# A template's bands loaded as 16-bit halves in six transfers, a first pass ahead of the loop, and a triangular mask by selection

## The reference, cut to what matters

```python
# 1. tokens: normalized template matching, one map per image
norm_t = ((flat - mu) / (sd + EPS)).reshape(C, th, tw) / patch_elements   # 31x31 template per channel
result = _dw_conv2d(image, norm_t[:, None], 1, pad)                       # correlation
m1, m2 = _dw_conv2d(image, mean_kern), _dw_conv2d(image * image, mean_kern)
result = (result / (sqrt(m2 - m1 * m1) + EPS)).mean(axis=1)
result = jnp.where(jnp.isnan(result), 0, result)                          # [16, 256, 256]
# 2. h = layernorm(h + attention(h)): 256 tokens of width 256 an image, 16 query and 8 key heads of 64
sim = tanh(q @ k.T / 50) * 50 / 8;  sim = where(causal, -max, sim);  out = softmax(sim) @ v
# 3. h = layernorm(h + ffn(h)): silu(x w1) * (x w2), two gelu layers of 1024, and back to 256
```

## Time and profile before

| | us |
|---|---|
| median of three runs | 2039.68 |
| profiled execution, its own time | 2037.89 |
| its span in the profile | 2036.2 |
| PE busy | 1841.0 (90%) |
| DVE busy | 1184.6 (58%) |
| ACT busy | 876.8 (43%) |
| POOL busy | 473.1 (23%) |
| PE in the first 80 us, by stretches of ten | 0, 3.0, 2.3, 10.0, 0.9, 1.9, 10.0, 1.9 |

### The profile page before, as it was taken

How to read it: one execution, slowest core, us unless ns; L and a number is a source line. 1 busy time by engine, 2 the same in 40 slices (tenths; PEclk the granted TensorE clock), 3 DMA queues, 4 the chain that set the end, 5 groups by cost and what they waited for, 6 DMA issues and landing times. The chain is left out here.

```text
span 2036.2 us, 31526 instructions
## 1 busy us (share of the span) xinstructions
PE 1841.0 (90%) x11768; PEld 1585.8 (78%) x11768; DVE 1184.6 (58%) x2083; ACT 876.8 (43%) x1076; POOL 473.1 (23%) x376
## 2 busy tenths in 40 slices
PE   3699999999969989998998999699999999999997
PEld 2698988988957877777787778578778787777876
DVE  6788788888865786776678676323241423414141
ACT  3655654545525764664576466122221222222221
POOL 2100000000022231221232123133433324333342
PEclk8799999999998999998999999799999999999999
DMA  8131222224001002000200100150000000000000
GB/s 168 49 128 49 96 78 90 76 99 143 22 32 63 23 15 77 24 15 9 85 23 15 56 22 22 49 223 14 8 21 0 21 0 21 21 0 21 0 11 12
DMA packets 17240, 96.81 MB, mean 48 GB/s; under 512 B 3270, under 2 KB 3398, under 8 KB 11209
## 3 DMA queue, kind: packets, MB, share of 16 engines
q1 hardware_dynamic: 17100, 94.90, 13.9%
HBM read 82.27 MB, written 24.15 MB: 52 GB/s over the span
## 5 line engine op out<-in xcount | busy, mean ns | idle before, releaser
L556 PE MATMUL conv<-w_hi,x_hi 128*128 128x368 f16 (+5 forms) x1320 | 355.8, 279 | 4.2 <-DVE planes L452 4.2
L556 PE MATMUL conv<-w_lo,x_hi 128*128 128x368 f16 (+5 forms) x1320 | 356.2, 279 | 0.0
L556 PE MATMUL conv<-w_hi,x_lo 128*128 128x368 f16 (+5 forms) x1320 | 355.0, 279 | 0.0
L818 POOL TENSOR_TENSOR probs<-probs,mask 128x512 f32<-128x512 f32 x128 | 166.8, 1303 | 444.1 <-ACT probs L892 444.1
L1310 ACT ACTIVATE raw_c<-ring,sh 128x512 f32<-128x512 f32 x128 | 88.2, 689 | 370.3 <-PE ring L1407 370.3
L1098 PE MATMUL mixed<-v,probs 128*128 128x65 f32 x1536 | 202.9, 283 | 41.5 <-DVE parts L978 41.5
L1098 PEld LDWEIGHTS mixed<-v,probs 128*128 128x128 f32 x1536 | 187.2, 197 | 56.8 <-issue 40.0
L1407 PE MATMUL ring<-ha_hi,wh 128*128 128x512 f32 x512 | 208.2, 407 | 16.9 <-POOL ha_lo L1272 16.9
L1272 POOL TENSOR_TENSOR ha_lo<-raw_c,ha_hi 128x512 fp32r<-128x512 f32 x128 | 165.0, 1289 | 210.1 <-DVE ha_hi L1322 210.1
L1407 PE MATMUL ring<-ha_lo,wh 128*128 128x512 f32 x512 | 205.4, 401 | 0.0
L1322 DVE CAST ha_hi<-raw_c 128x512 fp32r<-128x512 f32 x128 | 80.7, 631 | 212.9 <-ACT raw_c L1310 210.7
(11 more groups left out here) (148 smaller groups left out, 3563.7 us busy)
## 6 DMA issues: line engine op xcount, KB each, us to landing
xt<-x_columns_in SPq DMA_DIRECT2D x12, 1163.0 KB, 5.3
xp<-x_patches_in SPq DMA_DIRECT2D x12, 1152.0 KB, 5.2
hidden_words<-hidden_weights_in SPq DMA_DIRECT2D x8, 1408.0 KB, 8.2
words<-hidden_words SPq DMA_DIRECT2D x32, 352.0 KB, 3.1
wh<-hidden_words SPq DMA_DIRECT2D x2, 4096.0 KB, 21.1
tokens<-planes SPq DMA_DIRECT2D x4, 1024.0 KB, 3.9
lines<-tokens SPq DMA_DIRECT2D x4, 1024.0 KB, 5.4
h<-tokens SPq DMA_DIRECT2D x4, 1024.0 KB, 7.4
```

The lines of the kernel that those rows point to most:

```text
L556: ins = pe.matmul(out, xs[:, c, RI - 1 - i:RI - 1 - i + NR, :, x].rearrange("p r g -> p (r g)"), w, start=(t == 0), stop=(t == len(terms) ...
L818: pool.tensor_tensor(diag, diag, both, ALU.mult).then_inc(s_mask, 1)
```

## The change

It does four things.

1. The padded template is made as two 16-bit arrays of 47 rows of 64 (hi, and lo by a second DVE instruction), placed in the first 3 partitions of x_hi and x_lo, stored in two DMAs, and spread by six loads (one for each channel and half) over 128 partitions by 5,088 bytes. The casts on ACT and the subtractions on POOL go. Channel 0's two loads come before the loads of plane 1's image, channels 1 and 2 after them. The rows of a band in SBUF are 64 elements apart, not 48.
2. PE's `first()` runs the whole first group: in plane 0 correlate(0,0,0) comes after half of the turns, and the turns of plane 1 are moved back behind quarters 2 and 3; the loop begins at group 1. The order of the first pass on DVE and ACT changes with it, and POOL clears `lines` only after the template is normalized.
3. The mask is two selections of 256 columns (affine_select) in place of one product of 512.
4. `valid` is 16-bit.

```diff
-TROWS, TCOLS = TH + 16, TH + 32
+TROWS, TCOLS = TH + 16, TH + 33
+BAND = RI * PR * TCOLS
...
-            sp.wait_ge(s_tdve, 6)
-            sp.dma_start(TPAD, tpad).then_inc(s_tpad, 16)
-            sp.wait_ge(s_tpad, 16)
-            for c in range(CHANNELS):
-                for a in range(PR):
-                    size = (RI * PR - 1) * TCOLS + CJ * PC
-                    src = bass.AP(tensor=TPAD.tensor, offset=c * TROWS * TCOLS + a * TCOLS, ap=[[1, PC], [1, size]])
-                    sp.dma_start(spread[a * PC:(a + 1) * PC, c, 0:size], src).then_inc(s_wraw[c], 16)
+            for k in range(2):
+                sp.wait_ge(s_tdve, 6 + k)
+                sp.dma_start(TPAD[k], tpad[k]).then_inc(s_tpad, 16)
+            sp.wait_ge(s_tpad, 32)
+
+            def load_bands(c):
+                size = (RI * PR - 1) * TCOLS + CJ * PC
+                for k, w in enumerate((w_hi, w_lo)):
+                    src = bass.AP(tensor=TPAD.tensor, offset=(k * CHANNELS + c) * TROWS * TCOLS,
+                                  ap=[[TCOLS, PR], [1, PC], [1, size]])
+                    sp.dma_start(w[:, c, 0:size], src).then_inc(s_band[c], 16)
...
             def first():
+                load_bands(0)
                 load_xt(0, 1, 1)
                 load_x(0, 1, 1)
+                load_bands(1)
+                load_bands(2)
                 load_xt(0, 2, 2)
...
             def first():                      # ACT
                 square(0)
-                regroup(0)
                 split_hi(0, 0)
-                bands(0)
-                act.wait_ge(s_const, 5)
+                regroup(0, 0)
+                act.wait_ge(s_const, 7)
                 turned(0, 0)
-                turned(0, 1)
+                regroup(0, 1)
                 square(1)
                 mean_square(0)
-                bands(1)
-                regroup(1)
-                bands(2)
+                turned(0, 1)
+                regroup(1, 0)
+                act.wait_ge(s_tpad, 32)
                 deviation(0)
+                regroup(1, 1)
...
             def first():                      # DVE
                 sum_down(0, 0)
+                split_lo(0, 0)
                 sum_down(0, 1)
-                split_lo(0, 0)
-                dve.wait_ge(s_tpad, 16)
                 sum_across(0, 0)
+                sum_down(1, 0)
                 sum_across(0, 1)
-                sum_down(1, 0)
                 variance(0)
                 sum_down(1, 1)
-                dve.wait_ge(s_wlo, CHANNELS)
+                dve.wait_ge(s_tpad, 32)
...
             def first():                      # PE
-                turn_sums(0, range(8))
+                turn_sums(0, range(4))
+                correlate(0, 0, 0)
+                turn_sums(0, range(4, 8))
+                correlate(0, 0, 1)
+                correlate(0, 0, 2)
+                turn_sums(1, range(4))
+                correlate(0, 0, 3)
+                turn_sums(1, range(4, 8))
+                for c in range(1, CHANNELS):
+                    body(0, c, c, False)
...
-                        diag = probs[:, n % 4].rearrange("p m (b i) -> p m b i", b=3)[:, :, 0:3:2]
-                        both = mask[:].rearrange("p (m b i) -> p m b i", m=1, b=1).to_broadcast([P, 2, 2, P])
-                        pool.tensor_tensor(diag, diag, both, ALU.mult).then_inc(s_mask, 1)
+                        settle(pool, s_settle)
+                        for jb in range(2):
+                            diag = probs[:, n % 4, :, 2 * jb * P:(2 * jb + 1) * P]
+                            ins = pool.affine_select(out=diag, in_=diag, compare_op=ALU.is_ge, fill=0.0, base=0,
+                                                     pattern=[[0, 2], [1, P]], channel_multiplier=-1)
+                        ins.then_inc(s_mask, 1)
```

More of the change, by code:

```diff
@@ L106, in token_stage @@
         eps_t = sb("eps_t", [P, 1])
[L107 to L108 removed]
+        w_hi = sb("w_hi", [P, CHANNELS, BAND], F16)
+        w_lo = sb("w_lo", [P, CHANNELS, BAND], F16)
+        bands = lambda w: w[:].rearrange("p k (i a w) -> p k i a w", i=RI, a=PR)
         xp = sb("xp", [P, XW])
@@ L119, in token_stage @@
         guess = sb("guess", [P, PR, SIDE])
-        planes_4 = sb("planes_4", [P, 4, PR, SIDE])
-        valid, part, rinv, total = (planes_4[:, k] for k in range(4))
+        valid = sb("valid", [P, PR, SIDE], F16)[:]
+        planes_3 = sb("planes_3", [P, 3, PR, SIDE])
+        part, rinv, total = (planes_3[:, k] for k in range(3))
         tmpl = part[0:CHANNELS].rearrange("p a c -> p (a c)")[:, 0:TAPS]
         tsq = part[0:CHANNELS].rearrange("p a c -> p (a c)")[:, TAPS:2 * TAPS]
[L125 to L128, removed]
+        tpad = [x[0:CHANNELS, 1:].rearrange("p k r g c -> p (k r g c)")[:, 0:TROWS * TCOLS] for x in (x_hi, x_lo)]
         conv = psum("conv", [P, 4, 512])
@@ L138, in token_stage @@
         s_tpad = sem("s_tpad")
-        s_wraw = [sem("s_wraw%d" % c) for c in range(CHANNELS)]
-        s_whi = sem("s_whi")
-        s_wlo = sem("s_wlo")
+        s_band = [sem("s_band%d" % c) for c in range(CHANNELS)]
         s_xp = sem("s_xp")
@@ L165, in token_stage, with planes @@
         LAST = GROUPS * CHANNELS - 1
-        def planes(eng, body, first):
+        def planes(eng, body, first, start=0):
             first()
-            with eng.Fori(0, GROUPS - 1) as g:
+            with eng.Fori(start, GROUPS - 1) as g:
                 for c in range(CHANNELS):
@@ L235, in _ @@
         def _(pool):
+            for k in range(2):
+                pool.memset(tpad[k], 0.0).then_inc(s_const, 1)
+            pool.memset(eps_t[:], EPS_T).then_inc(s_const, 1)
             pool.memset(ident[:], 0.0).then_inc(s_const, 1)
-            pool.memset(tpad, 0.0).then_inc(s_const, 1)
+            pool.wait_ge(s_const, 4)
+            pool.affine_select(out=ident[:], in_=ident[:], compare_op=ALU.not_equal, fill=1.0, base=0,
+                               pattern=[[-1, P]], channel_multiplier=1).then_inc(s_const, 1)
+            pool.wait_ge(s_tdve, 6)
             pool.memset(sh.lines[:], 0.0).then_inc(s_const, 1)
             pool.memset(sh.neg_half[:], -0.5).then_inc(s_const, 1)
[L240 to L243, removed]
             def split_weights():
@@ L278, in square, with regroup @@
                 act.activation(xt_sq[:], xt[:], ACT.Square).then_inc(s_sq, 1)
-            def regroup(n):
-                for k in range(4):
-                    q, b = k // 2, k % 2
+            def regroup(n, q):
+                for k in range(2 * q, 2 * q + 2):
+                    b = k % 2
                     act.wait_ge(s_down, n * 4 + k + 2)
@@ L383, in _ @@
             dve.wait_ge(s_tdve, 5)
[L384 to L387, removed]
+            dve.wait_ge(s_const, 2)
+            raw = tmpl.rearrange("p (r c) -> p r c", c=TH)
+            inner = [pad.rearrange("p (r c) -> p r c", c=TCOLS)[:, PR:PR + TH, PC:PC + TH] for pad in tpad]
+            dve.tensor_scalar(inner[0], raw, tstat[:, 5:6], None, ALU.mult).then_inc(s_tdve, 1)
+            dve.wait_ge(s_tdve, 6)
+            dve.scalar_tensor_tensor(out=inner[1], in0=raw, scalar=tstat[:, 5:6], in1=inner[0],
+                                     op0=ALU.mult, op1=ALU.subtract).then_inc(s_tdve, 1)
             def sliding(out, line):
@@ L546, in correlate @@
                 terms = [(xx, i, xs, ws) for xx in cin for i in range(RI)
-                         for xs, ws in ((x_hi, w_hi), (x_hi, w_lo), (x_lo, w_hi))]
+                         for xs, ws in ((x_hi, bands(w_hi)), (x_hi, bands(w_lo)), (x_lo, bands(w_hi)))]
                 quarter = 4 * PC * b
@@ L571, in body @@
                 correlate(c, n, 3)
-            planes(pe, body, first)
+            planes(pe, body, first, 1)
 BANKS = 3
```

17 lines of the change are left out of this document (5 added, 12 removed).

## The result

The changed kernel took **1981.5 us** (median of four runs, 1977.19 to 1994.58), the kernel before 2040.63 beside it: ratio 0.9719, 95% interval 0.9691 to 0.9747. Five more runs later gave a median of 1982.57. The prediction was 1995, range 1976 to 2022, faster at 0.93. The profiled execution took 1977.19 us (span 1975.5), 60.7 less than the profiled one of before, against 44.8 predicted. The next paragraphs read this one execution; where another execution of the same code differs, the text says so.

A forecast was written before the change was run, and what follows sets the result against it. DVE and ACT in turn were taken to pace the token stage, DVE held up by POOL's mask to delay PE in attention. Head 24.8 plus mask 20 off 2037.9 gives 1993.1, median 1995 us; own range 1982 to 2006, stated 1976 to 2022.

The forecast's parts named there:

- Part 1: Start of the band loads: net between 2.5 us earlier and 1.2 later, taken as 0, so they go out at 13.4.
- Part 2: Band load speed: eight engines, 126 GB/s taken within 61 to 205, channel 0 complete at 26.0 us.
- half the engines at the old pace: Rival on the band loads: 61 GB/s, the head loses 3 us instead of gaining 25, total 2023; chance 0.15.
- Part 3: Head of the token stage: path to plane 0's first reciprocal sums to 53.6 us instead of 78.43, 24.8 us earlier.
- Part 4: Edits costed at nothing: 16-bit `valid`, band rows 64 apart, first group unrolled on PE, POOL's extra semaphore step.
- the ring: Token stage after the head: DVE and ACT in turn set the pace, 43.4 us a plane, PE following with little slack.
- Part 5: Mask in attention: two selections at 0.80 us a head instead of 1303 ns; 20 us together, bounds 3 and 35.
- shifted work meets new holds: Attention: reason for taking 15 us of PE idle time from the mask where the waits worked out at 19.
- Clock: Attention: PE's lower clock after waits of over 2 us; perhaps 5 of 15 us come back.
- it gives nothing: Rival on the mask: waits turn into DVE's own chain, or the price is 1.18 us; total 2012 to 2015; chance 0.10.
- it is slower: Rival on the mask: selections at the product's rate or worse on POOL, 1.3 us each, +25, 2065; chance 0.03.
- the case of faster loads: Rival on the band loads: 205 GB/s or more, head gains 28 us, total 1992; chance 0.12.

The follow-up runs named there:

- loads_of_16: The changed kernel with each of the six band loads cut into eight of 16 partitions (48 loads on 16 engines): 1978.93 us.
- turns_first: The changed kernel with PE turning all eight sums of plane 0 ahead of its first correlation, as before: 1984.84 us, ratio 0.9725 to the kernel before.
- bands_ahead: The changed kernel with all six band loads issued ahead of the second plane's image loads: 2001.11 us, ratio 0.9829 to the kernel before.
- no_mask: The changed kernel without POOL's mask selections, POOL only passing the semaphore on and diagonal blocks left unmasked: 1963.05 us.
- product_back: The changed kernel with the mask as one product of 512 columns again, nothing else undone: 2013.66 us, ratio 0.9873 to the kernel before.
- product_in_four: The changed kernel with the mask as four products of 128 columns, one for each 128x128 block: 2004.4 us.

## Why the prediction was right, and where it was off

**Part 1.** The bands go out at 12.52, 0.9 earlier than the 13.4 taken and inside the bounds.

**Part 2.** 126 GB/s taken, 122 measured, eight engines as read from the earlier trace rows; the first correlation at 26.22, predicted 26. The wide bounds (61 to 205) were honest, and the nearest row was the right choice. The rival of half the engines at the old pace fell: each engine went at twice its old pace, so most of the limit is shared, as loads_of_16 shows from the other side (twice the engines, 150 GB/s for 122).

**Part 3.** L426 predicted at 53.6, measured 55.06; gain 23.4 for 24.8. The missing us is in the first quarter: 9.1 taken, 10.3 measured (26.22 to the turns at 36.55), and it goes with PE's standing idle for 5.74 us ahead of it. Its first matmuls of 248 columns stand 0.21 us apart until 28.69, though the profile has a granted clock of 1.00, the upper level, for 26 to 31 us; from 34.36 on they stand 0.11 apart, and so they do in turns_first, where PE comes straight from transposes. The changed kernel, then turns_first:

```profile
28.26 0.42 PE L556 MATMUL conv<-w_lo,x_hi 128*128 128x248 f16 x1
28.47 0.42 PE L556 MATMUL conv<-w_hi,x_lo 128*128 128x248 f16 x1
```
```profile
27.65 0.27 PE L556 MATMUL conv<-w_hi,x_hi 128*128 128x248 f16 x1
27.76 0.27 PE L556 MATMUL conv<-w_lo,x_hi 128*128 128x248 f16 x1
```

Over the seven traces with this first pass and six loads L426 stands between 54.46 and 56.47, so the 53.6 was short by 1 to 3 us. That the gain needs the image load's place in the queue was the prediction's step, and bands_ahead gives 23.2 of 23.4 back. That casts and subtractions "give nothing by themselves" was argued in the prediction and is not shown. xt of plane 2 was to be landed at 56.5 and needed at 61.7; its scans start at 63.20, and DVE doesn't wait for it.

**Part 4.** `valid` takes 1.22 us, and the ring with the new band rows has its old period of 43.6 us. Nothing of them shows, as costed, but they were not tried one by one.

**Part 5, the term that was mis-sized.** 20 us predicted, bounds 3 and 35, measured 36.5 in the profiled executions, above the upper bound, and 32 to 35 in the medians. The price of a selection was right (0.80 us a head, 0.81 measured). The term that was too small is idle time: 15 taken, 26.7 measured. PE's wait for parts fell by 22.2 where I had worked out 19, and I then cut that to 15 for "shifted work meets new holds"; the new wait for the mask itself is 3.4, and other waits for DVE went too (for kt from 4.5 to 1.0; the row of before follows). The cut was a guess without a row, and wrong.

```profile
PE sim L1084 <- DVE kt L969: 4.5, 7, 1.0
```

The working also took DVE's sum for a measure of what stays, and reckoned a fifth of its loss; with the mean at 311 ns it is 2.3 of 37 us. The norms kept a third of theirs (9 of 27 us), and PE's wait goes with them. Clock: 5 taken from two stalls in each of three groups, 9.7 between the two profiled executions, but about 7 against the median of nine traces; a fourth of the idle time that went, near the third that I had reckoned. no_mask has more, 8.3 beside 8.1 of idle time, so the proportion isn't fixed. The rivals on the mask (it gives nothing; it is slower) fell with product_back.

In all: 1993.1 predicted for the profiled execution, 1977.2 measured; the 15.9 us between them are 16.5 more in part 5, 1.4 less in the head, and 0.8 in the MLP, which I had taken as it was. The median of 1981.5 lies just below the forecast's own range, 1982 to 2006. The stated range of 1976 to 2022 holds it, because that range takes in the case of faster loads too, which didn't come; that the understated mask fell into this room is luck.

## What to carry to other kernels

When a queue feeds two consumers, look first at what stands behind the bulk load: here the head's 23 us were gone when the old order of issue came back, with all the other edits kept. What one engine's long instruction costs another is set by how it falls on the other's chain of short instructions; replace it by a cheaper one or cut it short, but each piece pays its fixed part. Look for the instruction that the slowest engine waits for, and count what is lost ahead of it: the sum behind it recovered in product_in_four, and TensorE gained little. Idle time taken from TensorE can come back more than once where its clock follows it, but a single pair of traces can't price that: the same attention code took from 641.6 to 657.0 us of matmuls. A gain of under 5 us can hide in that spread; a store's issue time ahead of it is steadier, here within 3 us over eight traces.

## What the hardware showed that was not expected

- A load of 128 partitions with eight as outermost size ran at 112 to 124 GB/s, whatever its source; image loads split over 16 engines ran at 426, and their rows at 207 on the same eight engines.
- POOL's selection of 256 columns takes 407 ns at the median, a product of 512 takes 1303 in the mean and one of 128 takes 460 at the median: on a triangular mask the selection is much the cheaper.
- TensorE ran at its lower level for 20 us while 96% busy (turns_first, 1210 to 1230 us). What started it stays open.
- After 5.74 us of idle the matmuls from 26.22 to 28.69 us started at half the later pace while the profile's granted clock read 1.00; in loads_of_16 it is the same after 3.22 us of idle, from 23.70 on.
